# Three rows' first-layer experts on blocks of scattered tokens

## The reference

```python
shared_enc = _expert_stack(x, sW1, sb1, sW2, sb2).sum(0)     # 128 -> 512 -> 128
weights = jax.nn.softmax(x @ gW + gb, axis=-1)               # 15 experts
topv, topi = jax.lax.top_k(weights, 3)
gated = (jax.nn.one_hot(topi, 15) * topv[..., None]).sum(axis=-2)
router_out = _expert_stack(x, rW1, rb1, rW2, rb2)            # each 128 -> 256 -> 128, exact Gelu
return shared_enc + jnp.einsum('ebtd,bte->btd', router_out, gated) + x
```

## Time and profile before

| | us |
|---|---|
| median of 3 runs | 937.01 (936.86 to 939.99) |
| profiled execution, its time | 944.65 |
| profiled execution, span | 942.9 |
| PE busy | 781.0 (83%) |
| DVE busy | 651.1 (69%) |
| ACT busy | 533.4 (57%) |
| POOL busy | 245.3 (26%) |

### The profile page before, as it was taken

The page is one execution under the profiler, slowest core; times in us unless marked ns, Lnnn a source line. Parts: engine busy times, 40 slices in busy tenths (PEclk is TensorE's granted clock), DMA queues, the critical chain, the costliest instruction groups (busy, mean ns, idle before and its releaser), DMA issues. The chain is left out here.

```text
span 942.9 us, 12902 instructions
## 1 busy us (share of the span) xinstructions
PE 781.0 (83%) x4212; PEld 492.7 (52%) x4212; DVE 651.1 (69%) x1292; ACT 533.4 (57%) x976; POOL 245.3 (26%) x323
## 2 busy tenths in 40 slices
PE   4798888889987999999989789989989998338750
PEld 2454545445554677778767534444444443227740
DVE  5475586776672876866767696788988884438843
ACT  1345445546556677777767456656656666126740
POOL 3237655524421100000000230012212231144425
PEclk9589899999999999999999999999999999759985
DMA  5323411111100770000001121221321310021013
GB/s 167 68 62 90 85 25 31 36 36 35 27 10 1 224 223 0 1 1 1 1 12 22 31 62 34 43 72 24 83 43 37 89 25 13 0 74 45 29 37 87
DMA packets 56671, 46.84 MB, mean 50 GB/s; under 512 B 5831, under 2 KB 46620, under 8 KB 56604
## 3 DMA queue, kind: packets, MB, share of 16 engines
q1 hardware_dynamic: 55435, 43.72, 19.4%
q0 software_dynamic: 1024, 2.10, 0.8%
q10 hardware_dynamic: 144, 0.20, 0.1%
HBM read 14.67 MB, written 14.55 MB: 31 GB/s over the span
## 5 line engine op out<-in xcount | busy, mean ns | idle before, releaser
L923 ACT ACTIVATE ring<-single 128x512 f32<-128x512 f32 (+3 forms) x512 | 253.1, 518 | 196.8 <-PE single L1188 189.2
L1577 DVE TENSOR_REDUCE mneg<-pair 128x2 f32<-128x1024 f32 (+3 forms) x256 | 258.3, 1022 | 71.2 <-PE pair L1172 31.9
L1188 PE MATMUL single<-q_op,k_op 128*128 128x512 f32 (+3 forms) x512 | 215.7, 440 | 14.3 <-ACT ring L923 9.1
L1168 PE MATMUL pair<-k_op,q_op 128*128 128x512 f32 (+3 forms) x512 | 167.6, 406 | 13.0 <-DVE mneg L1577 11.4
L1188 PEld LDWEIGHTS single<-q_op,k_op 122*128 122x128 f32 (+1 forms) x512 | 96.8, 195 | 95.7 <-ACT ring L923 74.0
L1168 PEld LDWEIGHTS pair<-k_op,q_op 120*128 120x128 f32 (+1 forms) x512 | 98.2, 203 | 54.0 <-DVE mneg L1577 34.7
L1205 PE MATMUL p_o<-ring,vaug 128*9 128x512 f32 (+3 forms) x1024 | 114.0, 517 | 1.0 <-ACT ring L923 0.9
L1629 DVE TENSOR_TENSOR ring<-ring,single 128x1024 f32<-128x1024 f32 x60 | 73.2, 1221 | 46.9 <-ACT ring L952 45.4
L952 ACT ACTIVATE ring<-pair,cols 128x512 f32<-128x512 f32 x136 | 86.2, 686 | 32.5 <-PE pair L1252 26.7
L1634 DVE TENSOR_TENSOR hid_lo<-ring,hid_hi 128x1024 fp32r<-128x1024 f32 x68 | 83.3, 1224 | 22.9 <-ACT hid_hi L967 19.5
L967 ACT ACTIVATE hid_hi<-ring 128x1024 fp32r<-128x1024 f32 x68 | 72.2, 1062 | 31.3 <-issue 30.5
(11 more groups left out here) (311 smaller groups left out, 1347.7 us busy)
## 6 DMA issues: line engine op xcount, KB each, us to landing
xs<-zero SPq DMA_DIRECT2D x10, 1024.0 KB, 10.2
k_op<-hl SPq DMA_DIRECT2D x112, 64.0 KB
q_op<-hl SPq DMA_DIRECT2D x16, 256.0 KB
stage<-in_L_ffn_W_dram SPq DMA_DIRECT2D x8, 512.0 KB, 5.0
stage<-in_L_ffn_rW_dram SPq DMA_DIRECT2D x6, 512.0 KB, 4.9
q_op<-hl SPq DMA_DIRECT2D x48, 64.0 KB
xb<-xs SPq DMA_DIRECT2D x15, 128.0 KB, 2.0
xs<-yb SPq DMA_DIRECT2D x15, 128.0 KB, 1.7
```

What stands on the lines that cost most here:

```text
L923: exp_done.by(act.activation(ring[:, n % 8, lo:T], singles[n % 2][:, lo:T], ACT.Exp), (L, n))
L1168: ins = pe.matmul(both[:, i, 0:hi], r32(qs[:, P * qt:P * (qt + 1)]), r32(ks[:, 0:hi]), start=i == 0 or L == 1 or qt >= 2, stop=L == 1)
L1188: st_full.by(pe.matmul(singles[n % 2][:, lo:T], r32(ks[:, P * kc:P * (kc + 1)]), r32(qs[:, lo:T]), start=True, stop=True), (L, n))
L1577: s_taken.by(dve.tensor_reduce(mneg[:, G % 2, 2 * p:2 * p + 2, qt], both[:, :, 0:hi], axis=AX.X, op=ALU.max, negate=True), (L, m))
```

## The change

Rows 0 to 2 no longer run their routed experts densely. Their tokens are transposed back ("ht"), given a place in the area of each of their three experts ("rk", which the first layer now has too), and scattered to `xs` by 36 indirect DMAs on POOL during the attention of the next rows; the third row's during the fourth row's attention, whose parts are moved up (`LAST0`). DVE makes a table of blocks ("bt"). After the attention `routed_rows` runs 32 blocks of 256 places (the most that can be needed, whatever the router says): rows in, two transposes, first product, Gelu, rounding, and the second product with the hidden tiles as the stationary operand and the weights as the moving one, so that tokens come out on the partitions and no transposes back are needed: twelve matmuls of 128 columns. Eight input slots; POOL copies each block's weights (128x1024). The results go back to `xs`; POOL gathers three rows of them for each token (36 indirect DMAs), and DVE adds them, weighted, to x (`add_experts`, "c0" to "c2"). `dense` keeps 23 units: two shared halves for each of the rows 0 to 2, and all 17 for row 3. The store is cleared in 13 DMAs during rows 0 and 1 of the attention. POOL sets two thirds of the key constants before it waits for its first load, the last third behind the small memsets.

```diff
+SPARSE = NB - 1
+CAP0 = T * SPARSE // BLK
+ROOM0 = CAP0 * BLK
+NBLK0 = (TOP * T * SPARSE + E0 * (BLK - 1)) // BLK
+STORE = E0 * CAP0 + NBLK0 - TOP * T * SPARSE // BLK
+SLOTS = 8
...
+UNIT = [(r, u) for r in range(SPARSE) for u in (E0, E0 + 1)] + [(NB - 1, u) for u in range(UNITS)]
...
+BESIDE0 = {1: ["T.ot3"], 3: ["T.on"], 4: ["T.proj"], 6: ["T.ns"], 7: ["T.na"], 8: ["T.n1"], 9: ["T.n2"], 10: ["T.n3"], 11: ["T.ne"],
+           13: ["T.ln2"], 15: ["T.hin"], 16: ["T.lg"], 18: ["T.ex"], 20: ["T.rt1"], 22: ["T.rt2"], 24: ["T.gt"], 26: ["tb4"]}
+BESIDE = {7: ["c0"], 8: ["tb0"], 9: ["P.ns"], 10: ["P.na", "tb1"], 11: ["P.n1", "P.n2"], 12: ["P.n3", "P.ne"], 13: ["P.ln1"], 14: ["tb2"],
+          15: ["P.q"], 16: ["tb3"], 17: ["P.k", "c1"], 18: ["wo1"], 19: ["P.v"], 22: ["c2"]}
 for _r in range(NB):
...
+            def clear(n):
+                first = 8 * BLK * n
+                sp.dma_start(xs[first:first + 8 * BLK, :].rearrange("(p b) d -> p b d", p=P),
+                             w_qkv[:, 0:D].unsqueeze(1).broadcast_to([P, 16, D])).then_inc(zeroed, 16)
...
                 head_dma(G + 3)
-                if r == 1:
+                if r == 0:
                     sp.wait_ge(pool_set, 1)
+                    apart(sp)
+                if r < 2:
+                    clear(6 * r)
+                    clear(6 * r + 1)
...
+            def block_in(n):
+                if n >= SLOTS:
+                    xl0_ready.wait_ge(sp, n - SLOTS)
+                at = sp.value_load(btab0[0:1, 0, n:n + 1], min_val=0, max_val=STORE - 1)
+                sp.dma_start(xb0[:, n % SLOTS, :, :].rearrange("p t d -> p (t d)").unsqueeze(1), blocks_of[:, bass.ds(at, 1), :]).then_inc(xb0_in[n % SLOTS], 16)
...
+            pool.wait_ge(pool_set, 1)
+            steps.step(pool.memset(k_op0[96:P, 0:2 * GH, :], 1.0))
             pool.wait_ge(loads[3], n_load[3])
...
+            pool.memset(k_op0[96:P, 2 * GH:3 * GH, :], 1.0).then_inc(pool_set, 1)
+            pool.wait_ge(pool_set, 5)
...
+            def scatter0(s, i):
+                if i == 0:
+                    taken.wait_ge(pool, ("ht", s))
+                    taken.wait_ge(pool, ("rk", s))
+                    pool.wait_ge(zeroed, 16 * (STORE // 8))
+                    apart(pool)
+                t, k = i // TOP, i % TOP
+                pool.indirect_dma_start(xs, bass.IndirectOffsetOnAxis(ap=idx0[:, s, t, k:k + 1], axis=0), h_tok0[:, t, :], None).then_inc(scattered0, 16)
...
+                    if r in (1, 2) and k >= 28:
+                        for i in range(2 * (k - 28), 2 * (k - 28) + 2):
+                            scatter0(r - 1, i)
+                    elif r in (2, 3) and k in (4, 5):
+                        for i in range(2 * k, 2 * k + 2):
+                            scatter0(r - 2, i)
+                    elif r == 3 and 22 <= k < 28:
+                        for i in range(2 * (k - 22), 2 * (k - 22) + 2):
+                            scatter0(r - 1, i)
...
+            w0_of = w0[:, :, :, :, :].rearrange("p w s (e c) n -> p (w s) e (c n)", c=2)
+            b0_of = cols[:, R_B0:R_B0 + 2 * E0].rearrange("p (e c) -> p e c", c=2)
+            for n in range(NBLK0):
+                e = pool.value_load(btab0[0:1, 1, n:n + 1], min_val=0, max_val=E0 - 1)
+                if n >= 3:
+                    y0_full.wait_ge(pool, n - 3)
+                    apart(pool)
+                pool.tensor_copy(b_blk0[:, n % 3, :].unsqueeze(1), b0_of[:, bass.ds(e, 1), :])
+                w0_here.by(pool.tensor_copy(r32(wst0[n % 3][:, :, :].unsqueeze(2)), w0_of[:, :, bass.ds(e, 1), :]), n)
+                if n == 12:
+                    full.wait_ge(pool, ("proj", NB - 1))
+                    apart(pool)
...
+            def gather0(r):
+                for k in range(TOP):
+                    for t in range(NT):
+                        pool.indirect_dma_start(yg0[r][:, k, t, :], None, xs,
+                                                bass.IndirectOffsetOnAxis(ap=idx0[:, r, t, k:k + 1], axis=0)).then_inc(gathered0[r], 16)
...
+            y0_full.wait_ge(pool, NBLK0 - 1)
+            yb0_ready.wait_ge(pool, NBLK0 - 1)
+            for i in range(2):
+                pool.wait_ge(yb0_out[i], 16 * ((NBLK0 + 1 - i) // 2))
+            apart(pool)
...
+                def hidden(n):
...
+                    for c in range(2):
+                        ins = act.activation(hid0[:, n % 2, c, :], pairs[n % 2][:, 0, BLK * c:BLK * (c + 1)], ACT.Gelu, bias=b_blk0[:, n % 3, c:c + 1])
+                    gelu0_done.by(ins, n)
+                    gelu0_done.wait_ge(act, n)
+                    if n >= 2:
+                        y0_full.wait_ge(act, n - 2)
+                    apart(act)
+                    e0_hi.by(act.activation(r32(hid0_hi[:, n % 2, :, :]), hid0[:, n % 2, :, :], ACT.Copy), n)
...
+                def first_layer(n):
+                    xl0_ready.wait_ge(pe, n)
+                    w0_here.wait_ge(pe, n)
...
+                    for c in range(2):
+                        dst = pairs[n % 2][:, 0, BLK * c:BLK * (c + 1)]
+                        hi, lo = (r32(wst0[n % 3][:, half, P * c:P * (c + 1)]) for half in range(2))
+                        pe.matmul(dst, hi, r32(xt0_hi[:, n % 2, :]), start=True, stop=False)
+                        pe.matmul(dst, hi, r32(xt0_lo[:, n % 2, :]), start=False, stop=False)
+                        ins = pe.matmul(dst, lo, r32(xt0_hi[:, n % 2, :]), start=False, stop=True)
+                    e0_full.by(ins, n)
...
+                def second_layer(n):
...
+                    for t in range(2):
+                        dst, at = (p_o, p_m)[n % 2][:, P * t:P * (t + 1)], slice(P * t, P * (t + 1))
+                        for c in range(2):
+                            hi, lo = (r32(wst0[n % 3][:, 2 + half, P * c:P * (c + 1)]) for half in range(2))
+                            pe.matmul(dst, r32(hid0_hi[:, n % 2, c, at]), hi, start=(c == 0), stop=False)
+                            pe.matmul(dst, r32(hid0_hi[:, n % 2, c, at]), lo, start=False, stop=False)
+                            ins = pe.matmul(dst, r32(hid0_lo[:, n % 2, c, at]), hi, start=False, stop=(c == 1))
...
+                rows_in(0)
+                for n in range(NBLK0 + 2):
+                    if n + 1 < NBLK0:
+                        rows_in(n + 1)
+                    if n < NBLK0:
+                        first_layer(n)
+                    if 1 <= n <= NBLK0:
+                        second_layer(n - 1)
+                    for name, b in beside_block(n):
+                        part(name, b)
...
+            def add_experts(r):
+                y = yg0[r]
+                dve.wait_ge(gathered0[r], 16 * TOP * NT)
+                taken.wait_ge(dve, ("tb4", NB - 1))
+                apart(dve)
+                for t in range(NT):
+                    ins = dve.tensor_scalar(y[:, 0, t, :], y[:, 0, t, :], gate0[:, r, t, 0:1], None, ALU.mult)
+                step(ins)
+                for k in range(1, TOP):
+                    for t in range(NT):
+                        ins = dve.scalar_tensor_tensor(out=y[:, 0, t, :], in0=y[:, k, t, :], scalar=gate0[:, r, t, k:k + 1], in1=y[:, 0, t, :],
+                                                       op0=ALU.mult, op1=ALU.add)
+                    step(ins)
+                step(dve.tensor_tensor(y[:, 0, :, :], y[:, 0, :, :], tab0[:, r:r + 1, :].broadcast_to([P, NT, D]), ALU.mult))
+                added0.by(dve.tensor_tensor(x_row(r), x_row(r), y[:, 0, :, :].rearrange("p t d -> p (t d)"), ALU.add), r)
```

More of the change, by code:

```diff
@@ L202, in every_part @@
                 out += beside_quad(a, q, "b") + beside_quad(a, q, "d")
-        out += [part for v in range(DSTEPS) for part in beside_unit(v)] if L == 0 else drain_parts()
+        if L == 0:
+            out += [part for n in range(NBLK0 + 2) for part in beside_block(n)]
+            out += [part for v in range(DSTEPS) for part in beside_unit(v)]
+        else:
+            out += drain_parts()
     return out
@@ L246, in build @@
         guard = put("guard", [P, 2, 2, NB])
-        w_q = [put(f"w_q{L}", [P, P]) for L in range(2)]
-        w_k1 = put("w_k1", [P, P])
+        w_q0 = put("w_q0", [P, P])
         w_abs = put("w_abs", [P, 256])
@@ L368, in build @@
         h_hi_ready, h_lo_ready = sig("h_hi_ready", order_of("hin")), sig("h_lo_ready", order_of("hin"))
-        units = list(range(NB * UNITS))
+        units = list(range(len(UNIT)))
         hid_full, gelu_done = sig("hid_full", units), sig("gelu_done", units)
-        routed = [v for v in units if v % UNITS < E0]
+        routed = [v for v in units if UNIT[v][1] < E0]
         spread, gated = sig("spread", routed), sig("gated", routed)
@@ L430, in tiles @@
             return ap.rearrange("p (t n) -> p t n", t=NT)
-        in_units = {part for v in range(DSTEPS) for part in beside_unit(v)}
+        in_units = {part for v in range(DSTEPS) for part in beside_unit(v)} | {part for n in range(NBLK0 + 2) for part in beside_block(n)}
```

(24 more changed lines are left out.)

342 lines of the change are left out of this document (253 added, 89 removed), and 7 rows, old and new, of tables (LAST0, TABLE).

## The result

The changed kernel takes 961.06 us (median of 4 runs, 960.70 to 967.98), beside 937.53 for the kernel before (936.86 to 939.99, 4 runs): ratio 1.0256, 95% interval 1.0215 to 1.0297. It is 23.5 us slower, where 8 us faster was forecast. Its profiled execution has a span of 959.0 and took 960.70.

What follows compares the result with a forecast made beforehand. TensorE was taken to bound the feed-forward stage, with DVE close behind. Lead -5, scatters +19, ranks +4, clears +3 and stage -29 gave -8 us: from the median of 937.0 to 929, range 908 to 960.

Steps and rivals of the forecast that it cites:

- Lead: Kernel start: POOL's key-constant memset holds DVE's scale of modT; reordering it gains 4.9 us, between 3 and 5.
- Scatters: First layer's attention: scatters on POOL delay its cuts, costing 19 us (8 to 26): 10 at two row changes, 9 in row four.
- Clears: Attention rows 0 and 1: clears issued ahead of small transfers delay a few of them, costing 3 us (0 to 12).
- Ranks and copies: First layer's attention: ranks and token copies for three rows, about 1.3 us of TensorE a row, costing 4 us (2 to 8).
- Blocks: Stage behind the attention: 32 blocks at 3.0 us, plus filling and the fourth row's remaining parts, take 110 us.
- rival (a): Blocks: 128-column products take 0.23 us or 0.29, not 0.12, so TensorE bounds them; 954 us, slower; chance 0.27.
- Dense rest: Remaining dense units and fourth row: 101 us, including weighted sums on DVE of which 11 us come through.
- rival (c): Gathers behind the blocks: DVE passes hold them, so the sums wait; +16 us, 945; chance 0.10.
- Stage: Stage behind the first layer's attention, blocks plus dense rest: 211 us instead of 240, so -29.
- Rival (d): First layer's attention loses more than thought, by unrecovered lag or clears ahead of the maxima: +10 us, 939; chance 0.10.

Runs made afterwards that it cites:

- e1_lead: The kernel before with only the new order of the key constants' memset: 935.77 us, ratio 0.9982.
- e4_clears_early: The kernel before with its clears moved to rows 0 and 1 of the attention, 13 for 10, and some second-layer loads and weight splitting a row later: 955.40 us, 1.0186.
- e2_no_scatters: The changed kernel without its 36 scatters, so the blocks work on cleared rows: 943.15 us, ratio 1.0053.
- e15: The changed kernel with only the weighted sums cut in nine pieces and moved, the third sum into the second layer's first row: 952.78 us, ratio 1.0135.
- e16: The changed kernel with only the part behind the ranks moved half a quad or more away from them: 959.44 us, ratio 1.0232.
- e5: The changed kernel without scatters and with the fourth row's parts at the other rows' quads, no longer moved up: 938.79 us, ratio 0.9993.
- e10: The changed kernel without the weighted sums, only the last addition to x kept: 945.84 us, ratio 1.0073.
- e6: The changed kernel with the same 13 clears, each behind the heads' transfers and mostly one at a time: 963.68 us, ratio 1.0259.
- e7: The changed kernel with its clears at the same places in pieces of 1536 bytes in place of 512: 961.20 us, ratio 1.0229.
- e9: The changed kernel with its clears issued on ACT's queue, one every second quad of rows 0 and 1: 962.89 us, ratio 1.0288.
- e11: The changed kernel with one scatter a half quad and the clears on ACT's queue in 1536-byte pieces: 950.02 us, ratio 1.0157.
- e14: e11 plus GpSimd's weight copy waiting for DVE's subtraction, the part behind the ranks moved, and the weighted sums in nine pieces: 926.83 us, ratio 0.9880.
- e3: The changed kernel with one scatter behind each of twelve half quads in place of two behind six: 954.24 us, ratio 1.0165.

## Why the prediction was wrong

From the traces, in us: the starts of the last value product and of the second layer's first maximum, and the span.

| kernel | last value product | second layer starts | span |
|---|---|---|---|
| e1_lead | 286.3 | 525.5 | 933.6 |
| e4_clears_early | 304.1 | 544.8 | 953.7 |
| e2_no_scatters | 315.3 | 529.6 | 937.2 |
| changed | 334.2 | 549.0 | 959.0 |

The attention is 47.9 longer, the stage behind it 24.4 shorter, what comes then 1.9 longer, which I can't explain: +25.4 (959.0 - 933.6). Of the 47.9, 17.7 are the clears (e4), 19.0 the scatters (changed less e2), and 11.2 are left for ranks and copies (e2 less e4). These are differences of single traces, and those differ by 6.5 us already at the end of the first row, which is the same work in the changed kernel (112.1) and in e15 (118.6).

- **Lead, -4.9.** Wrong as a term against the median: 1.7. The mechanism is right, GpSimd's memset holds DVE, but only where it starts first, and the profiled execution happened to have it 0.11 us ahead. A loss that hangs on a tenth of a microsecond should have been weighted, and the 7.6 us between that execution and the median said that something in it was unusual. Moving the whole sum over to the median counted this twice.
- **Scatters, +19.** Right in sum and mechanism: 2.85 a half quad for 2.93, 19.0 in all. Its parts are off: 7.8 and 10.3 at the row changes, where I had 5 each, and 5.7 in the fourth row, where I had 9 (changed less e2, by quarters; the two traces differ by 4.8 the other way before the first scatter). So the exact 19 is in part luck.
- **Clears, +3 (0 to 12).** The step that failed most: 17.4. I had written that "behind two of them a transfer lands some 7 to 10 us later; most have that much slack, one or two a row don't", and priced the misses at next to nothing. One late transfer of keys costs TensorE 4.84 us in one wait, and three quarters of the two rows have a loss of 4 to 7. The clears of the earlier trace rows were free where they stood: from 293 to 367 TensorE of the kernel before waits for no transfer. "Nobody waits for them" is true in both kernels; what I left out is who waits for the transfers beside and behind them.
- **Ranks and copies, +4 (2 to 8).** 11, as what is left. I counted TensorE's products. What costs, as far as the traces show, is DVE's chain behind them. The waits of TensorE in e2, which has ranks and copies but no scatters, 130 to 270 us:

```profile
PE p_m L1257 <- DVE idx L1802: 4.1, 2, 2.1
PE pair L1358 <- DVE mneg L1885: 3.5, 5, 1.2
...
PE p_m L1257 <- DVE onorm L1721: 2.2, 2, 1.1
```

  e4, with the same clears, has neither the first nor the third there, and 3.3 of the second.

  e16 shows that moving what waits for idx isn't enough (2 us, since onorm is then waited for), e5 that the parts moved up in the fourth row are some 5. The remaining 5 or so stay unassigned: in the fourth row's third quarter of e2 (287.3 to 304.6) DVE is busy 12.9 of 17.3 us, where e1 (263.5 to 276.4) has 8.2 of 12.9, and TensorE's clock is 0.75 there where e1's is 1.00.
- **Blocks, 110.** 107.8 (to the end of their last product, 442.03). Products of 128 columns at 0.11 (I took 0.12), so rival (a) is refuted. The Trainium skill's 81 ns for them (TensorE: Matmul & The Clock Gate, Back-to-back issue gap) isn't reached in this kernel. A block costs 3.13 (32 Gelus from 340.66 to 437.55), my 3.0. But the handovers aren't all of it: TensorE is busy 93.7 of 107, at a clock of 0.87.
- **Dense rest, 101.** 106.9. The weighted sums come through whole (some 15 in the traces and 17 by the ratio of e10, not 11), because each stands in one piece on DVE in front of work that TensorE waits for. Of rival (c) a little is true: the second row's twelve gathers take 18.6 us beside a busy DVE (462.91 to 481.5), 1.55 each and not 1.26; nothing waits for them. Its premise was misread: gathers of the second layer do run beside a busy DVE in the kernel before, as the one at 922.96, 0.95 long, beside a sum from 923.09 to 924.23; they weren't held there.
- **Stage, -29.** -24.4.

Sum of the misses: lead 3.2, clears 14.4, ranks 7.2, stage 4.6, the end 1.9, together 31.3 of the 32 between 929 and 961. Rival (d), "the attention loses more than I think", named the right place, and the clears in it, with 10 us at a chance of 0.10; it was 22.

TensorE's clock is not a term by itself here. The granted clock is 0.50 (1.2 GHz) from 308 to 349 in the changed kernel, where TensorE had stood 2.2 us for DVE up to 308.7 and then waits 3.8 us for GpSimd's cuts, and 1.00 (2.4 GHz) from 122 to 336 in e1, where no wait before its last value product is longer than 1.3. It is in the prices above: in e4 some 10 us more of waits go with 17.7 us of loss and a lower clock.

## What to carry to other kernels

Price bulk transfers that move from an idle stage into a busy one by the latest small transfer beside them, and ask what one late one costs the engine in order behind it; moving 13 MB beside the attention cost nearly as much as all 36 scatters (17.4 and 19.0 us). Work that is hidden "by share" on an in-order engine must be cut to the size of the gap it is to hide in: the same sums cost 17 us in three blocks, and nine pieces gave 11 of them back (e15). Before a stall in a trace is booked as a gain, look at how near the two starts are, and at how that execution stands to the median.

## What the runs showed of the hardware

- Another queue, another order or pieces three times as long, each alone, didn't make 1 MB clears measurably cheaper for the small transfers beside them (e6, e7, e9: 1.0229 to 1.0288 against 1.0256, intervals of 0.004 to 0.006). A queue of their own and long pieces together come with shorter waits of TensorE for transfers (e11 to e14: 4.5 to 4.9 us between 40 and 200; e3: 7.8).
- A memset on GpSimd, which reads nothing, held a DVE operation of 128x4 elements for 5.13 us when it started 0.11 us earlier, and didn't when it started 0.26 us later (e4: 0.22 us). Small DVE steps are held by GpSimd's rope copies too: 1.33 us for one of 128x4 at 194.61 in the changed kernel, beside a copy from 194.53 on, and 0.16 for the same at 196.36.
- A gather issued by GpSimd takes 0.94 us at 465.15 in the changed kernel, and 1.60 to 1.98 where it starts 0.06 to 0.44 us behind DVE's subtraction of 128x1024 (462.91, 466.39, 470.80 and 478.27).
- Rounded 32-bit products of 128 columns start 0.11 us apart with their weight loads, nearly like those of 256 columns (0.12).
